# A two-chain scan over key blocks: joined 256-column products, rounded key rows and a new order of a turn

## The reference, cut

```python
kv = x @ W_KV;  k, v = split(kv)          # 1024 steps of 2 rows each, 128 features
def loss_fn(params, k_t, v_t):            # _mlp: silu(h @ W1 + b1) @ W2 + b2
    return jnp.mean((_mlp(params, k_t) - v_t) ** 2)
def step(params, kvt):
    g = jax.grad(loss_fn)(params, k_t, v_t)
    return tuple(p - LR * gp for p, gp in zip(params, g)), None
params, _ = jax.lax.scan(step, (W1, b1, W2, b2), (k, v))
return _mlp(params, x @ W_Q)
```

## Time and profile before

| | us |
|---|---|
| median of 3 runs (lowest, highest) | 511.83 (509.27, 514.12) |
| the profiled execution, its own time | 513.47 |
| its span | 511.6 |
| busy: TensorE matmul, weight load | 441.3, 363.6 |
| busy: VectorE, ScalarE, GpSimd | 277.3, 245.3, 233.8 |

### The profile page before, as it was taken

One profiled execution on the slowest core, in us unless ns is written; L12 is line 12 of the kernel. 1 busy time (PEld: TensorE's weight loads), 2 busy tenths in 40 slices (PEclk: granted clock), 3 DMA queues, 4 the chain that ended last, 5 costly groups with the idle time before them and its releaser, 6 DMA issues.

```text
span 511.6 us, 10071 instructions
## 1 busy us (share of the span) xinstructions
PE 441.3 (86%) x2962; PEld 363.6 (71%) x2962; DVE 277.3 (54%) x1045; ACT 245.3 (48%) x650; POOL 233.8 (46%) x335
## 2 busy tenths in 40 slices
PE   7896787999935999999999999999986869999950
PEld 5342477999932578999999999974532468999940
DVE  4852334555528556666666666655871443555524
ACT  2872134555530355556556556535871324555520
POOL 4176575444530033545545545551066665544430
PEclk9999999999975999999999999999998799999985
DMA  8961316101036500000000000000011316101019
GB/s 232 282 221 42 94 49 182 36 27 31 10 91 173 131 1 1 1 1 3 2 1 2 1 3 1 1 1 2 2 37 47 100 43 188 33 27 31 24 35 228
DMA packets 34515, 30.91 MB, mean 60 GB/s; under 512 B 3838, under 2 KB 30085, under 8 KB 34464
## 3 DMA queue, kind: packets, MB, share of 16 engines
q1 hardware_dynamic: 24608, 19.17, 13.7%
q0 software_dynamic: 4544, 8.47, 5.2%
q10 hardware_dynamic: 5312, 2.62, 1.9%
HBM read 15.55 MB, written 15.61 MB: 61 GB/s over the span
## 4 chain that ended last, share of the span: by engine, by line
PE 75%; DVE 9%; issue 5%; DMA 4%; another core or an unknown queue 3%; ACT 2%; POOL 1%; ACTq 1%; DVEq 0%; POOLq 0%
PE bank L1220 20%; PE bank L701 15%; PE bank L688 14%; PE bank L659 4%; PE bank L559 3%; DMA stage<-y_dram 3%; PE bank L649 3%; PE bank L1043 2%; PE bank L676 2%; PE bank L1108 2%; PE bank L1076 2%; PE bank L1081 2%; DVE stats L409 1%; PE bank L1102 1%
## 5 line engine op out<-in xcount | busy, mean ns | idle before, releaser
L1600 DVE TENSOR_TENSOR sq<-bank,relu 128x512 f32<-128x512 f32 x86 | 59.4, 691 | 106.5 <-ACT relu L801 73.6
L1350 POOL DMA_INDIRECT y_dram<-y_out,stage x78 | 76.4, 980 | 71.3 <-ACT y_out L827 66.1
L701 PE MATMUL bank<-proj_w,sq 128*128 x624 | 88.1, 285 | 12.1 <-DVE sq L1600 7.3
L1345 POOL DMA_INDIRECT slots_dram<-rows,slots x64 | 63.3, 989 | 67.5 <-ACT rows L752 35.4
L701 PEld LDWEIGHTS bank<-proj_w,sq 128*128 128x128 f32 x624 | 77.0, 194 | 16.7 <-issue 14.8
L688 PE MATMUL bank<-tileT,tile_w 128*128 128x128 f32 x624 | 83.9, 279 | 2.9 <-ACT tileT L793 2.8
L801 ACT ACTIVATE relu<-bank 128x512 f32<-128x512 f32 x94 | 55.8, 595 | 53.3 <-PE bank L688 25.2
L688 PEld LDWEIGHTS bank<-tileT,tile_w 128*128 128x128 f32 x624 | 77.3, 195 | 3.4 <-ACT tileT L793 3.1
L827 ACT ACTIVATE y_out<-bank,stage 128x128 f32<-128x128 f32 x78 | 28.7, 367 | 48.2 <-PE bank L701 38.2
L1215 POOL TENSOR_TENSOR sq<-sq,last_rows 128x128 f32<-128x128 f32 x32 | 14.6, 456 | 50.1 <-DVE sq L1196 50.1
L559 PE MATMUL bank<-ones 128*128 128x512 f32 x38 | 22.1, 730 | 15.5 <-DVE res L1651 12.7
(11 more groups left out here) (269 smaller groups left out, 1061.6 us busy)
## 6 DMA issues: line engine op xcount, KB each, us to landing
slots_dram<-pad SPq DMA_DIRECT2D x2, 2535.0 KB, 13.9
stage<-slots_dram SPq DMA_DIRECT2D x18, 260.0 KB
fc_w<-experts SPq DMA_DIRECT2D x1, 2048.0 KB, 20.3
proj_w<-experts SPq DMA_DIRECT2D x1, 2048.0 KB
stage<-y_dram SPq DMA_DIRECT2D x8, 256.0 KB, 5.5
stage<-y_dram ACTq DMA_DIRECT2D x8, 256.0 KB, 6.1
y_dram<-y_out,stage POOLq DMA_INDIRECT x78, 2.6
res<-x SPq DMA_DIRECT2D x4, 256.0 KB, 4.2
```

The costliest lines, as they stand in the source:

```text
L701: last = nc.tensor.matmul(bank[4 + i % 2][:, 0:P], sq[:, i % 2, f_cols], proj_w[:, k, f_cols], start=j == 0, stop=j == FJ - 1)
L1345: nc.gpsimd.indirect_dma_start(to, bass.IndirectOffsetOnAxis(slots[:, n:n + 1], 0), rows[:, k, b, :], None, bounds_check=limit, oob_is_err ...
L1350: nc.gpsimd.indirect_dma_start(y_dram.ap(), bass.IndirectOffsetOnAxis(tiles[:, t, P:P + 1].bitcast(U32), 0), y_out[:, t % YBUFS, :], None, ...
L1600: nc.vector.tensor_tensor(wide_of(i)[2], wide_of(i)[0][:], wide_of(i)[1], ALU.mult)\
```

## The change

In the ahead chain, products with the same stationary side become one product with 256 moving columns. `w2_ident` holds ahead_w2 beside the identity, so that one product with stationary a gives the guess and the transposed a in one bank; `e_w2t` holds e beside ahead_w2t, so that one product with stationary e gives e·e and the slope product; offset and old slope product get 128 more columns (zeros, `ident_zero`, `zero_rows`) so that both halves of the bank belong to one sum. One copy on ScalarE (`act_guess_rows`) takes guess and transposed a out together. The transposed th moves to bank 0 and e·e to bank 2, with new waits for that. The key rows are also kept rounded (`k_rows_r`, four casts on GpSimd in the prologue), and the ahead chain's w1 sums use them. The order of a turn is new on TensorE, ScalarE and VectorE, and so is that of the parameters' moves (`PARAMS`). The final chain's products are the same ones.

```diff
-        rounded = sb("rounded", [P, 2, T], F32R)
+        rounded = sb("rounded", [P, 3, T], F32R)
...
+        k_rows_r = rounded[:, 2, :].rearrange("p (b d) -> p b d", d=P)
...
+        w2_ident = sb("w2_ident", [P, 3 * P], F32R)
+        ahead_w2, ident_r, ident_zero = w2_ident[:, 0:P], w2_ident[:, P:2 * P], w2_ident[:, P:3 * P]
+        e_w2t = sb("e_w2t", [P, 2 * P], F32R)
+        ahead_e, ahead_w2t = e_w2t[:, 0:P], e_w2t[:, P:2 * P]
+        guess_rows = sb("guess_rows", [P, 3 * P + 2], F32R)
+        ahead_guess, zero_rows, ahead_rows = guess_rows[:, 0:P], guess_rows[:, P:3 * P], guess_rows[:, 2 * P:3 * P + 2]
...
+            elif part == 3:
+                pool.wait_ge(krows_copied, g + 1)
+                nc.gpsimd.tensor_copy(k_rows_r[:, g * GRP:(g + 1) * GRP, :], k_rows[:, g * GRP:(g + 1) * GRP, :])\
+                  .then_inc(krowsr_done, 1)
...
-        PARAMS = ("w1", "b2", "b1", "b1_half", "ahead_w1", "w2t", "w2", "ahead_b1", "ahead_b1_half",
-                  "ahead_w2t", "ahead_b2", "ahead_w2")
+        PARAMS = ("w1", "b1_half", "b1", "b2", "w2t", "w2", "ahead_w1", "ahead_b1_half", "ahead_b1", "ahead_b2",
+                  "ahead_w2t", "ahead_w2")
...
         def pe_first(pe, step, turn):
...
-                pe.wait_ge(x.th_done, step.n)
+                pe.wait_ge(x.u_done if x is ahead else x.th_done, step.n)
...
         def pe_offset(pe, step, turn):
...
+            if x is ahead:
+                if step.n:
+                    pe.wait_ge(x.erows_done, step.n)
+                wait_param(pe, step, turn, "w2")
+                nc.tensor.matmul(x.t_bank[:, 0:2 * P], x.offset, ident_zero, start=True, stop=False)
...
         def pe_yrows(pe, step, turn):
...
+            if x is ahead:
+                nc.tensor.matmul(x.t_bank[:, 0:2 * P], x.a, w2_ident[:, 0:2 * P], start=False, stop=True)\
+                  .then_inc(x.yrows_done, 1)
...
         def pe_da_old(pe, step):
...
+            if x is ahead:
+                pe.wait_ge(x.guess_done, step.n + 1)
+                pe.wait_ge(x.d_done, step.n)
+                nc.tensor.matmul(x.d_bank[:, 0:2 * P], x.ee[:, old.to, :], zero_rows, start=True, stop=False)
+                return
...
         def pe_da(pe, step):
...
-            mm(x.d_bank, x.e, x.w2t, start=step.old is None).then_inc(x.da_done, 1)
+            if x is ahead:
+                nc.tensor.matmul(x.d_bank[:, 0:2 * P], x.e, e_w2t[:], start=step.old is None, stop=True)\
+                  .then_inc(x.da_done, 1)
...
         def pe_w1_sums(pe, step, done):
...
-            weights = mm(x.d_bank, k_rows[:, step.block, :], x.ed[:, step.to, 1, :].bitcast(F32))
...
+            if x is ahead:
+                pe.wait_ge(x.ee_done, step.m + 1)
+                mm(x.d_bank, k_rows_r[:, step.block, :], x.ed[:, step.to, 1, :])
...
+        def act_guess_rows(act, step):
+            x = step.chain
+            act.wait_ge(x.yrows_done, step.n + 1)
+            nc.scalar.copy(guess_rows[:, 0:3 * P].rearrange("p (a d) -> p a d", d=P)[:, 0::2, :],
+                           x.t_bank[:, 0:2 * P].rearrange("p (a d) -> p a d", d=P)).then_inc(x.guess_done, 1)
...
+            pool_key_part(pool, 3, 0)
...
                 dve_w1(turn)
+                dve_b1(turn)
                 if early:
                     dve_d(dve, early[1])
...
-                dve_biases(turn)
+                dve_b2(turn)
...
+            pe.wait_ge(krowsr_done, NG)
```

More of the change, by code:

```diff
@@ L1016, in pe_offset @@
             pe.wait_ge(offset_done, 2 * step.block + (1 if x is ahead else 2))
-            if step.n:
-                pe.wait_ge(x.d_done, step.n)
-            wait_param(pe, step, turn, "b1_half" if x is ahead else "w1")
-            mm(x.d_bank, x.offset, ident_r[:], stop=False)
+            if x is ahead:
[3 more added lines that the diff above has]
+                nc.tensor.matmul(x.t_bank[:, 0:2 * P], x.offset, ident_zero, start=True, stop=False)
+            else:
+                if step.n:
+                    pe.wait_ge(x.d_done, step.n)
+                wait_param(pe, step, turn, "w1")
+                mm(x.d_bank, x.offset, ident_r, stop=False)
         def pe_old_guess(pe, step):
@@ L1026, in pe_old_guess @@
             pe.wait_ge(old.chain.aa_done, old.m + 1)
-            mm(x.d_bank, old.chain.aa[:, old.to, :], old.chain.ed[:, old.to, 0, :], start=False, stop=False)
+            mm(x.t_bank if x is ahead else x.d_bank, old.chain.aa[:, old.to, :], old.chain.ed[:, old.to, 0, :],
+               start=False, stop=False)
         def pe_yrows(pe, step, turn):
@@ L1038, in pe_aa @@
             pe.wait_ge(x.a_done, step.n + 1)
-            if step.m:
+            if x is ahead and step.n:
+                pe.wait_ge(x.e_done, step.n)
+            if x is final and step.m:
                 pe.wait_ge(x.ee_done, step.m)
             if x is final:
-                wait_param(pe, step, turn, "b1_half")
+                wait_param(pe, step, turn, "b1")
             nc.tensor.matmul(x.y_bank[:, P:2 * P], x.a, x.a, start=True, stop=True)
@@ L1105, in pe_e_transposed @@
             x = step.chain
-            pe.wait_ge(x.u_done, step.n + 1)
+            if x is final:
+                pe.wait_ge(x.u_done, step.n + 1)
             pe.wait_ge(x.e_done, step.n + 1)
@@ L1116, in pe_w1_sums @@
             pe.wait_ge(x.d_done, step.n + 1)
-            weights = mm(x.d_bank, k_rows[:, step.block, :], x.ed[:, step.to, 1, :].bitcast(F32))
-            if x is final:
-                weights.then_inc(done, 1)
+            if x is ahead:
+                pe.wait_ge(x.ee_done, step.m + 1)
+                mm(x.d_bank, k_rows_r[:, step.block, :], x.ed[:, step.to, 1, :])
+            else:
+                mm(x.d_bank, k_rows[:, step.block, :], x.ed[:, step.to, 1, :]).then_inc(done, 1)
         def pe_b1_sums(pe, step, done):
@@ L1134, in pe_w2t_sums @@
             x = step.chain
-            nc.tensor.matmul(x.t_bank[:, P:2 * P + 2], x.ed[:, step.to, 0, :], x.rows[:], start=True, stop=True)\
+            nc.tensor.matmul(x.t_bank[:, P:2 * P + 2], x.ed[:, step.to, 0, :], x.rows[:, 0:P + 2], start=True, stop=True)\
               .then_inc(done, 1)
@@ L1194, in dve_u @@
             x = step.chain
-            dve.wait_ge(x.rows_done, step.n + 1)
-            nc.vector.scalar_tensor_tensor(x.u, x.rows[:, 0:P].bitcast(F32), 1.0, x.t_bank[:, P:2 * P], ALU.subtract,
+            if x is ahead:
+                dve.wait_ge(x.guess_done, step.n + 1)
+                dve.wait_ge(x.t_done, step.n + 1)
+            else:
+                dve.wait_ge(x.rows_done, step.n + 1)
+            th_rows = (x.h_bank if x is ahead else x.t_bank)[:, P:2 * P]
+            nc.vector.scalar_tensor_tensor(x.u, x.rows[:, 0:P].bitcast(F32), 1.0, th_rows, ALU.subtract,
                                            ALU.mult).then_inc(x.u_done, 1)
@@ L1202, in dve_d @@
             dve.wait_ge(x.slope_done, step.n + 1)
-            nc.vector.scalar_tensor_tensor(x.ed[:, step.to, 1, :], x.slope, 1.0, x.d_bank[:, 0:P], ALU.subtract,
+            da = x.d_bank[:, P:2 * P] if x is ahead else x.d_bank[:, 0:P]
+            nc.vector.scalar_tensor_tensor(x.ed[:, step.to, 1, :], x.slope, 1.0, da, ALU.subtract,
                                            ALU.mult).then_inc(x.d_done, 1)
@@ L1546, in dve_w1, with dve_b1, dve_b2 @@
                 moved_by(final.w1, final.d_bank[:, 0:P], 0.5 * GRAD, final.w1)
-            def dve_biases(turn):
+            def dve_b1(turn):
+                f = final
+                dve.wait_ge(upd1_done, 2 * turn + 2)
+                moved_by(f.b1_half, f.y_bank[:, P:P + 1], 0.25 * GRAD, f.b1_half)
+                moved_by(f.b1, f.y_bank[:, P:P + 1], 0.5 * GRAD, f.b1)
+            def dve_b2(turn):
                 f = final
@@ L1896, in _ @@
                     pe_da(pe, early[0])
+                    pe_first(pe, early[1], turn)
                     pe_e_transposed(pe, early[0])
-                    pe_ee(pe, early[0])
                 pe_y_old(pe, late[1])
@@ L1901, in _ @@
                 if early:
-                    pe_first(pe, early[1], turn)
                     pe_again(pe, early[1])
-                    pe_offset(pe, early[1], turn)
                 pe_y_last(pe, late[1])
```

143 lines of the change are left out of this document (68 added, 75 removed).

## The result

| | before | after |
|---|---|---|
| median (lowest, highest), 20 runs of each | 511.75 (509.27, 514.47) | 508.59 (506.15, 512.87) |
| ratio of the two, 95% interval | | 0.9938 (0.9920 to 0.9956) |
| profiled execution, its span | 513.47, 511.6 | 507.87, 506.1 |
| a turn | 9.54 | 9.29 |

The change is faster by 3.2 us, not by the 9.2 that were forecast: a turn lost 0.25 us and not 0.60. Of the 5.5 us between the two spans 1.53 are not counted as a gain of the change: the first product of the ahead steps starts at 173.54 instead of 175.07, ahead of every edited product. From there to the scan's first product it is 17.71 us after and 17.91 before, 0.20 less; the turns (first products of block 0 to 15) take 139.46 instead of 142.89, 3.43 less.

The account below looks back on a forecast made before the run. TensorE's queue was taken to bound the scan: 0.5 from records plus 0.1 from order a turn, fifteen turns 9.0, less 0.1, plus 0.3 prologue, made 9.2 us, so a median of 502.6, range 497.5 to 512.

Parts of the forecast that it names:

- The records: TensorE's queue: joined products save 0.42 us, rounded sums 0.11, three wider products cost 0.03; 0.50 us a turn less.
- Four times two records become one: 4 x (0.224 - 0.12) = 0.42 us less: Ahead chain's two rounds: each of four product pairs, 0.224 us, becomes one joined product of 0.12.
- The order: Start of a turn on TensorE: new order gains 0.2 us, a later b2 takes half; 0.1 gained, between -0.3 and +0.5.
- stall of 0.32 on ahead_w1: Turn's start on TensorE: the early block's product ends 0.32 us after the sums instead of 0.11, with a·a behind it.
- Half of the 0.2 may go there: Turn's start: b2 and ahead_w1 come about 0.3 us later, which may take half of the new order's 0.2 gain.
- The widened copy: ScalarE: two copies become one of 256 columns, 0.375 us by a straight line; costed at nothing, at worst 0.11 a round.
- Rival 1: Relief spent in waits: only records just ahead of the final chain's next product help; 0 to 0.33 a turn, 506.5 to 511.5; chance 0.14.
- 0.96 of the 1.04: First product to round two's slope product: a full turn takes 7.73 us, the last 6.77, most of the final chain's 1.04 queueing.
- Rival 2: All queueing on TensorE goes: a turn reaches 8.50 us, 15.6 us gained, about 496; chance 0.08.
- Rival 3: Joining saves nothing: first way, a rounded record costs only 0.06, 511.8; second, 256 columns at f32 pace, 515; chance 0.06.
- Rival 4: ScalarE's final guess copy waits for the early block's silu beyond 0.65 us of slack; up to 518; chance 0.10.
- The tolerance loop: Rounded key rows move the ahead w1 beyond tolerance, so 1024 single steps run and time leaves every range; chance 0.02.

Follow-up runs that it names:

- e7: Changed kernel plus one unread spare transposed product of 128 columns in each of two rounds; 512.57 us, ratio 1.0013 to the kernel before, 9.42 a turn.
- e8: Changed kernel plus one unread spare product of the error with itself in each of two rounds; 512.75 us, ratio 0.9983 to the kernel before, 9.40 a turn.
- e12: Changed kernel with four unread spare products and the plain f32 key rows back, five records; 513.23 us, ratio 1.0039 to the kernel before, 9.60 a turn.
- e3: Changed kernel with plain f32 key rows again in the ahead chain's w1 sums; 512.59 us, ratio 0.9978 to the kernel before, 9.36 a turn.
- e6: Changed kernel with all four ahead sums before the offset product and masked e·e before b2; 508.60 us, ratio 0.9912 to the kernel before, 9.19 a turn.
- e9: As e6, with round two's joined guess product ahead of the final chain's old slope product; 507.20 us, ratio 0.9927 to the kernel before, 9.11 a turn.
- e10: As e9, with w2t sums before the ahead slope product, b1 behind, likewise on VectorE; 505.92 us, ratio 0.9901 to the kernel before, 9.10 a turn.
- e4: Kernel before with only rounded key rows added in the ahead chain's w1 sums; 514.94 us, ratio 1.0002 to the kernel before, 9.42 a turn.

## Why the prediction was too large

**What bounds it.** The reading that TensorE's queue decides and that waits hide in its rows was right in kind, but the forecast took the queue as one number. It is a queue with waits at fixed places. A record in front of such a wait was worth nothing where the final chain needed no product between the two at once (round one, e7 and e8). It was worth all of its 0.11 to 0.13 where it did (round two): in e7 the slope product stands there, in e8 the final sums, on which b2, the mask and so the end of the wait itself hang.

**The records: 0.50 forecast, 0.31 measured.** Their price on the queue was right (the joined product ends 0.11 behind its neighbour; 72 records a turn, though with 8.47 us of weight loads and not 8.3). That the slope product came 0.49 earlier, within the 0.4 to 0.6 forecast, is luck: 0.28 of it is the order (before to e12), 0.21 the records (e12 to after). Of the four joined pairs, however, only the two of round two count (e7 0.13, e8 0.11); the two of round one lie ahead of waits for the final chain's e and silu. The step that failed is "Four times two records become one: 4 x (0.224 - 0.12) = 0.42 us less", taken as time of the turn: it gave 0.24. With the sums' record, 0.08 in place (e3) and not 0.11, it is the 0.31 of e12, within rounding.

**The order: 0.1 gained forecast, 0.06 lost measured**, inside the -0.3 to +0.5 that were allowed for. The stall of 0.32 on ahead_w1 is gone, and a·a stands 0.30 behind its silu (257.30 against 256.64 + 0.36) instead of 0.50. But silu itself ends 2.63 after the slope product where it was 2.44 (260.24 - 257.80). The later b2 was named, and its size was right: the offset starts 0.36 later against the slope product, 0.3 was forecast (the sums for b2 had followed the w2 and the w1 sums, though, and not the w1 sums alone). The failing step is its price, "Half of the 0.2 may go there". The new wait of the sums for the masked e·e, which stands behind b2, was not in the forecast at all: it takes the place of the one removed, with TensorE's ends 0.35 apart (256.52 and 256.87) where the old stall had 0.32. From before to e12 the seam lost 0.18 to all that, and the way gained 0.12.

**The sum.** 0.31 - 0.06 = 0.25 a turn instead of 0.60. The turns give 3.43 us, the prologue 0.20 (0.3 forecast): 3.6, and the medians 3.2. The widened copy takes 0.37 us as estimated (below), and the ahead chain's first products of the scan did not wait for the casts.

```profile
L1207 ACT CAST guess_rows<-bank 128x256 fp32r<-128x256 f32 x33 | 12.4, 374 | 13.3 <-PE bank L1055 13.3
```

**The rivals.** Rival 1, the relief spent in waits, is what happened: its 0 to 0.33 a turn and 506.5 to 511.5 hold the 0.25 and the 508.6, and its argument was the true one, though it named round one's ee where round two's counts. It had a chance of 0.14. What spoke against it, that 0.96 of the 1.04 are lost by round two's slope product, was correct as a length, but not all of that stretch is places where records count (0.21 of the 0.49 won there is theirs), and it says nothing of the seam behind it. Rival 2 has no ground left: the final chain alone still takes 8.53 (330.71 to 339.24) where a turn takes 9.29. Rival 3 is excluded, its second way by the joined product's 0.11, its first by e7 and e8, where a record by itself costs 0.13 and 0.11 and not 0.06. Rival 4 did not come: the final guess is copied by 249.41 (249.15 + 0.26) and the masked a·a, which the same inner product needs, by 249.44, so the guess is still not what it waits for last; but of the 0.65 of slack 0.03 is left. The tolerance loop did not run. The rows of rival 4, ScalarE and VectorE, and of the last turn:

```profile
249.15 0.26 ACT L1201 COPY last_guess<-bank 128x128 f32<-128x128 f32 x1
...
249.15 0.29 DVE L1228 SCALAR_TENSOR_TENSOR last_aa<-bank,nmask 128x128 f32<-128x128 f32 x1 [0.34 <-PE bank L1275]
```
```profile
330.71 0.39 PE L1275 MATMUL bank<-stage,w_sb 128*128 128x128 f32 x2
...
339.24 0.43 PE L1275 MATMUL bank<-w_sb,wq_sb 128*128 128x128 f32 x2
```

**What sets the seam.** Behind the end of the final slope product the mask ends at 2.06 in after, at 1.96 to 1.97 in e6, e9 and e10, and at 2.17 in e8; in all five the sums start 0.14 to 0.15 later and a·a 0.69 to 0.73 after that, which is the seam of each. So the seam follows the mask, which in after and e8 is held up by the b2 move ahead of it on VectorE; in e10 b2 comes early, and the seam is that of e9. This is read from the rows; no run moved the mask alone.

**Open.** It was not tried to drop the sums' wait for the mask by another bank: the eight are taken.

## What to carry to other kernels

Do not price a record on a busy in-order queue by its length alone: go to the next place behind it where the engine waits for another one, and call the record free only if the chain that closes the loop needs no product between the two at once. The stall alone is no proof: two of the four spares stood ahead of a stall and cost their full length. Where a kernel is a loop, cut a turn at a product of the chain that closes it and make the sum for each part, the seam too, because an earlier middle is given back there when the parameters for the next turn come no earlier. A spare record put back in one place is the cheapest way to learn what a record there is worth; and a joined product and the order it needs are one edit, not two.

## What the runs showed of the hardware

In some profiled executions the first turn of the scan took about 1.4 us longer (10.32 in e4, 10.39 in e6, 10.71 in e12, against 8.98 in after), with records of 128 columns about 0.21 instead of 0.11 us apart for some 3 us. Stretches around the start of the scan, after and then e6, columns as in the earlier trace rows; those of after are laid 0.29 later, since its scan starts that much later (191.25 against 190.96):

```profile
189.29:192.29 3.00, 1.67 (x14) 1.37 (x12) 1.63 (x8) 1.10 (x4) 1.69 (x3) 1.00 0.00 0
192.29:195.29 3.00, 3.00 (x24) 2.83 (x25) 1.48 (x6) 1.74 (x7) 0.46 (x1) 1.00 0.00 0
```
```profile
189.00:192.00 3.00, 1.67 (x14) 1.37 (x12) 1.63 (x8) 1.10 (x4) 1.69 (x3) 1.00 0.00 0
192.00:195.00 3.00, 3.00 (x16) 3.00 (x17) 0.58 (x2) 1.47 (x6) 0.46 (x1) 0.56 0.00 0
```

In both, TensorE was busy for the same 1.67 of the 3 us ahead, at the prologue's end. In e6 it then had a granted clock of 0.56, mostly the lower level of 1.2 GHz; in after it kept 2.4 GHz. The Trainium skill, "TensorE: Matmul & The Clock Gate", "What's actually happening", says that the clock follows how busy the engine has been and that the same kernel differs from run to run in where this falls. The traces agree with the second; what decides between the two cases they do not show. Six of the fourteen profiled kernels show a first turn above 10.3. It is 0.3% of a run, as much as a few of the edits here, and is outside the turn of the table: compare turns of the trace before medians where less than one per cent matters.
